# Four more warming matmuls at the start of a one-core kernel of six network blocks

## The reference

```python
x = x + 0.5 * _L0_ffn_ref(_layernorm(x))       # channel mix: r * (relu(k)^2 W_v), inputs mixed with the previous token
x = x + _L0_attn_ref(_layernorm(x))            # 16 heads of 64, relative position bias, full softmax
x = x + 0.5 * _L0_ffn_ref(_layernorm(x))       # the same channel mix again
x = x + 0.5 * _L1_ffn_ref(_layernorm(x))       # two layers: local window attention (8 heads) + gated MLP
x = x + _L1_attn_ref(_layernorm(x))            # gated linear recurrence over the tokens, then a norm
x = x + 0.5 * _L1_ffn_ref(_layernorm(x))       # the two local layers again
```

```python
def _layernorm(x, axis=-1, eps=1e-05):
    m = jnp.mean(x, axis=axis, keepdims=True)
    v = jnp.var(x, axis=axis, keepdims=True)
    return (x - m) / jnp.sqrt(v + eps)
```

## Time and profile before

| | us |
|---|---|
| median of three runs | 1206.97 |
| lowest, highest | 1205.64, 1207.45 |
| profiled execution, device time | 1206.97 |
| its span, first to last instruction | 1205.2 |
| TensorE busy | 1145.7 (95%) |
| VectorE busy | 906.6 (75%) |
| ScalarE busy | 885.3 (73%) |
| GpSimd busy | 609.5 (51%) |
| mean granted clock of TensorE | 0.993 |

### The profile page before, as it was taken

The page is one execution under the profiler, slowest core; times in us unless marked ns, Lnnn a source line. Parts: engine busy times, 40 slices in busy tenths (PEclk is TensorE's granted clock), DMA queues, the critical chain, the costliest instruction groups (busy, mean ns, idle before and its releaser), DMA issues.

```text
span 1205.2 us, 39867 instructions
## 1 busy us (share of the span) xinstructions
PE 1145.7 (95%) x15770; PEld 697.1 (58%) x15770; DVE 906.6 (75%) x2419; ACT 885.3 (73%) x2390; POOL 609.5 (51%) x402
## 2 busy tenths in 40 slices
PE   7899999999999999799999999988999899999997
PEld 3345555655555554576666666554556566666664
DVE  2498888888889877786777777767677777777773
ACT  5666666666667668787977897777878688877874
POOL 0176665666656553564655564433435355554640
PEclk9999999999999999999999999999999999999999
DMA  5622222222323222310211111110111111110110
GB/s 174 240 61 65 73 65 72 60 78 55 82 56 81 56 56 84 101 42 19 49 41 22 38 43 30 22 29 18 40 27 32 32 28 41 41 41 20 41 41 19
DMA packets 35481, 66.71 MB, mean 55 GB/s; under 512 B 6704, under 2 KB 8176, under 8 KB 35296
## 3 DMA queue, kind: packets, MB, share of 16 engines
q1 hardware_dynamic: 35296, 64.16, 20.2%
HBM read 15.32 MB, written 1.11 MB: 14 GB/s over the span
## 4 chain that ended last, share of the span: by engine, by line
PE 79%; DVE 5%; ACT 5%; issue 4%; DMA 3%; SPq 3%; POOL 1%; DVEq 0%; ACTq 0%; POOLq 0%
PE ps L479 11%; PE ps L458 9%; PE ps L1437 7%; PE ps L1400 5%; PE ps L1367 5%; PE ps L1337 5%; PE ps L1316 5%; PE ps L1306 4%; PE ps L1407 4%; PE ps L1379 4%; PE ps L1307 3%; DMA arena<-arena 2%; PE ps L1443 2%; PE ps L487 2%; PE ps L444 2%
## 5 line engine op out<-in xcount | busy, mean ns | idle before, releaser
L417 POOL TENSOR_TENSOR arena<-arena 128x1024 f32<-128x1024 f32 x128 | 241.4, 1895 | 163.8 <-DVE arena L661 163.8
L568 ACT ACTIVATE arena<-arena 128x512 f32<-128x512 f32 x256 | 182.5, 714 | 118.4 <-DVE arena L647 118.4
L1248 POOL TENSOR_TENSOR arena<-arena 128x1024 f32<-128x1024 f32 x64 | 121.5, 1898 | 230.5 <-DVE arena L1819 230.5
L1641 ACT ACTIVATE arena<-arena 128x128 f32<-128x128 f32 x512 | 198.3, 391 | 30.6 <-DVE arena L1811 30.1
L647 DVE CUSTOM_DVE_ANT_0 arena<-ps,arena 128x512 f32<-128x512 f32 x256 | 164.6, 688 | 30.8 <-PE ps L458 28.0
L1811 DVE CUSTOM_DVE_ANT_0 arena<-ps,near,arena 128x128 f32<-128x128 f32 x512 | 144.4, 346 | 42.2 <-PE ps L1367 42.1
L657 DVE STREAM_TRANSPOSE arena<-arena 128x1024 f32<-128x1024 f32 x128 | 156.6, 1232 | 1.2 <-POOL arena L417 0.9
L479 PEld LDWEIGHTS ps<-arena 32*64 32x64 f32 x8192 | 120.3, 130 | 56.7 <-issue 31.8
L1255 POOL TENSOR_TENSOR arena<-arena 128x1024 f32<-128x1024 f32 x64 | 151.1, 2361 | 0.6 <-PE ps L1337 0.5
L458 PE MATMUL ps<-arena 64*128 64x512 f32 x512 | 142.1, 630 | 5.2 <-issue 3.5
L479 PE MATMUL ps<-arena 32*64 32x128 f32 x8192 | 137.5, 273 | 4.5 <-issue 2.7
(11 more groups left out here) (178 smaller groups left out, 2112.1 us busy)
## 6 DMA issues: line engine op xcount, KB each, us to landing
arena<-arena SPq DMA_DIRECT2D x191, 128.0 KB, 2.4
arena<-arena SPq DMA_DIRECT2D x64, 192.0 KB, 2.6
arena<-rel_rows SPq DMA_DIRECT2D x16, 448.0 KB, 9.0
arena<-arena SPq DMA_DIRECT2D x64, 64.0 KB, 2.1
arena<-y SPq DMA_DIRECT2D x30, 128.0 KB, 2.3
arena<-arena SPq DMA_DIRECT2D x15, 127.8 KB, 2.4
arena<-in_wqkv SPq DMA_DIRECT2D x2, 768.0 KB, 5.2
x<-in_x SPq DMA_DIRECT2D x4, 256.0 KB, 5.6
```

The lines of the kernel that those rows point to most:

```text
L417: nc.gpsimd.tensor_tensor(e, e, scale, ALU.mult).then_inc(self.normed, 1)
L568: nc.scalar.activation(self.e[:, r % 3, i, :], self.neg[:, i, :], ACT.Exp, bias=self.nmax[:, i:i + 1], scale=-1.0, accum_out=self.sums[:, ...
L1641: nc.scalar.activation(self.e[:, s, h, :], self.neg[:, h, :], ACT.Exp, bias=self.nmax[:, h:h + 1], scale=-1.0, accum_out=self.sums[:, s, h ...
```

## The change

`WARM` goes from 10 to 14, so that TensorE runs 14 and not 10 of the matmuls on zeros before it waits for the loads.

```diff
@@ -48,7 +48,7 @@
 LA_QK, LA_V, LA_S, LA_PT, LA_O = 2, 4, 0, 5, 7
 NEVER = 1.0e25
 TINY = 1.0e-24
-WARM = 10
+WARM = 14
 LOG_LIMIT = 1.0e19
```

## The result

| | us |
|---|---|
| before, median of 14 runs | 1205.71 (1199.91 to 1207.45) |
| changed, median of 14 runs | 1212.7 (1206.85 to 1217.52) |
| ratio | 1.0066, 95% interval 1.005 to 1.0084 |
| changed, profiled execution | 1210.86, span 1209.1, mean clock 0.989 |

Forecast was 1207.0 with a range of 1204.8 to 1208.6. The time lies outside it, and 0.66% is more than three times the 0.2% that the forecast called the limit of measurement. The medians lie 7.0 us apart; the ratio, applied to 1206 us, gives 8.0.

What follows compares the result with a forecast made beforehand. TensorE's matmuls were taken to bound the kernel, but waits for loads, VectorE's preparations and ScalarE's table load its opening. With the 0.71 us delay hidden, 1206.97 + 0 gave 1207.0 us, range 1204.8 to 1208.6.

Steps and rivals of the forecast that it cites:

- Price and place of the eight passes: Opening: eight passes cost 2.15 us at full clock, L128 starts 0.71 us late, all hidden under VectorE's preparations and table load.
- No gain from the warmer clock in the opening: Opening: clock already full from 7.7 to 24.68 us despite the idle times, so the passes gain 0.
- + 0: Whole kernel: the change's net effect in the sum, 0 us added to 1206.97 us.
- Rival three: Opening: late clock rise makes warming outlast its cover and delay L128; 1208.5 us, or 1211 with no rise; chance 0.04.
- Rival two: L230, at 24.68 us: added activity keeps the clock up, 3.0 us less, 1204.0 us; chance 0.04.
- Rival one: First normalization: in other executions the idle gap drops the clock; filling it saves about 2 us, about 1205.0; chance 0.10.

Runs made afterwards that it cites:

- Long10: Kernel before with its ten warming matmuls widened from 320 to 448 columns, no instructions added: 1204.57 us, ratio 0.9997 to the kernel before.
- pad4: Kernel before with four tiny matmuls (32 weight columns, 16 columns) added behind its ten warming matmuls: 1213.98 us, ratio 1.0064.
- w14pad12: Changed kernel (fourteen warming matmuls) with twelve tiny matmuls added behind them, 64 TensorE instructions more than before: 1204.0 against 1204.65 us, ratio 1.0005 to the kernel before.
- w8c400: Kernel before with eight warming matmuls of 400 columns instead of ten of 320, 8 instructions fewer: 1205.36 against 1202.01 us, ratio 1.0022.
- pad16: Kernel before with sixteen tiny matmuls added behind its ten warming matmuls, 64 TensorE instructions more: 1206.81 us, ratio 1.0016.

## Why the prediction was wrong

- Price and place of the eight passes: right, with some luck in the end of the warming, as the rise of the clock and the loads both came earlier than in the profile it was read from. The passes end behind the loads and under VectorE's preparations and the table load; L132 isn't late. Long10 shows it by itself, 0.9997.
- No gain from the warmer clock in the opening: right. L230 still begins at the low clock.
- The step that failed is the opening of the part on the change: "It adds four matmuls of 320 columns, so eight passes. Nothing is removed, no other engine's instructions change, no DMA and no semaphore is added." It counted what the matmuls take and left out that they move the 30,000 TensorE instructions behind them by 16 against the blocks in which instructions arrive. The "+ 0" of its sum was to be about +7 to +8 us (0.66%); by pad4's division some 2 of them from the stops and 6 from a lower clock, which falls behind some of the stops. "Only the opening matters here", in the part on the reference, went wrong in the same way.
- Rival three had the right side with the wrong mechanism: L128 behind the warming was never late. Rival two didn't happen (L230 is no quicker for it). Rival one shows nowhere: no profile has a low stretch between 11 and 20, and w14pad12 and long10 fill the idle time before L128 too and gain nothing.
- The profile of before could have warned: the earlier trace rows have over 15,000 TensorE passes, and the stops stand in its timeline too, as idle time put down to "issue" (0.74 us at 198.9), at a place where it costs little. I read the opening only.
- The range was taken from three runs of before and too narrow even for the kernel before; its 14 runs reach from 1199.91 to 1207.45, 35 others of it, timed beside w14pad12, from 1201.04 to 1211.24.

Open: why the packet starts late at just that end, why 16 fewer costs twice what 16 more does (its second stop in four units is a part of it), w8c400's 0.22% and pad16's 0.16%. That a stop brings the fall of the clock was seen in sequence in four profiles, not shown: no run kept the stops and took the falls away. No version beat the kernel before: of six positions tried, its own is the best.

## What to carry to other kernels

An instruction that costs nothing where it stands still moves everything behind it on its engine. Where a long stretch of very short instructions follows, look for idle time put down to "issue" at equal counts of instructions, and try the same change with a few empty instructions more, until the repeating pattern stands against the blocks as it did (here 64 instructions more in all, as 64 divides both the unit's 576 and the block's 256); only then is the time that of the change. A small edit ahead of such a stretch is to be timed in pairs (time without instructions, instructions without time) before anything is said of its cause.

## What the runs showed that I had not expected

- Instructions of TensorE arrive in packets of 16.3 KB, 256 instructions, each while the block ahead of it runs, and where one comes late TensorE stops: at the larger stops about 1 to 2.3 us from one start to the next. Within passes of 590 ns that shows as up to 0.74 us idle (before), within L479's passes, of which one starts every 16 ns (124 in 2.06 us), as up to 1.9.
- With 64 instructions more the time comes back (1.0005), with 16 more (1.0064) or 16 fewer (1.0137) it doesn't.
- The low stretches of the clock in the opening stood at other times in two profiles of one and the same program: from 24.68 in one, from 22.1 in the other.
